# Two graph layers on one core: small products ahead of the first columns, each bucket's norm and tables two groups further up

## The reference, cut to what matters

```python
edge_index = jnp.stack([src, dst])
# first layer: sums over the edges, then a residual norm
w0_features = x @ w0
w1_features = x @ w1
dst, src = (edge_index[0], edge_index[1])
messages = w1_features[src]
neighbours = jax.ops.segment_sum(messages, dst, num_segments=N)
x = _layernorm(x + jax.nn.relu(w0_features + neighbours))
# second layer: attention over the edges, a softmax per destination
h_all = jnp.einsum('nf,rof->rno', x, W).reshape(r, n, h, d)
h_src = h_all[edge_type, src]
h_dst = h_all[edge_type, dst]
scores = jnp.einsum('ehd,hd->eh', h_src, attn_src) + jnp.einsum('ehd,hd->eh', h_dst, attn_dst)
...
x = _layernorm(x + out.reshape(n, h * d))
```

## Time and profile before

| what | value |
|---|---|
| median of 3 runs | 2725.85 us (2725.09 to 2735.58) |
| profiled execution | 2729.65 us, span 2727.8 us |
| mean granted TensorE clock | 0.89 of full speed |
| busy share: TensorE, GpSimd, VectorE, ScalarE | 84%, 68%, 70%, 61% |
| chain that ended last: TensorE, VectorE, GpSimd, issue, DMA | 47%, 16%, 15%, 11%, 7% |

### The profile page before, as it was taken

One profiled execution on the slowest core, in us unless ns is written; L12 is line 12 of the kernel. 1 busy time (PEld: TensorE's weight loads), 2 busy tenths in 40 slices (PEclk: granted clock), 3 DMA queues, 4 the chain that ended last, 5 costly groups with the idle time before them and its releaser, 6 DMA issues.

```text
span 2727.8 us, 38107 instructions
## 1 busy us (share of the span) xinstructions
PE 2283.6 (84%) x9936; PEld 1648.0 (60%) x9936; DVE 1923.1 (70%) x4221; ACT 1656.4 (61%) x3517; POOL 1844.3 (68%) x1875
## 2 busy tenths in 40 slices
PE   8886798999999999999986677777777777777765
PEld 3465576677777777767764455555555555555541
DVE  9993765555555555555552788888888888888887
ACT  4594465566666666666645566666666666666643
POOL 1004777777777777777754777777777777777735
PEclk9996898999999999999997788888787788877888
DMA  5203455854444444444454445444554454444535
GB/s 159 80 5 112 115 158 135 251 175 153 162 154 162 154 152 147 159 155 154 162 122 162 130 140 148 139 139 140 145 142 139 137 148 141 137 139 138 142 91 160
DMA packets 177777, 387.53 MB, mean 142 GB/s; under 512 B 42669, under 2 KB 106867, under 8 KB 171042
## 3 DMA queue, kind: packets, MB, share of 16 engines
q0 software_dynamic: 83888, 233.09, 30.1%
q1 hardware_dynamic: 86626, 99.05, 12.3%
q10 hardware_dynamic: 7056, 52.99, 5.1%
HBM read 302.96 MB, written 82.03 MB: 141 GB/s over the span
## 4 chain that ended last, share of the span: by engine, by line
PE 47%; DVE 16%; POOL 15%; issue 11%; DMA 7%; DVEq 2%; ACT 1%; SPq 0%; POOLq 0%; ACTq 0%; PEldq 0%
PE ps L1689 21%; PE ps L1806 11%; PE ps L1741 10%; POOL region L1337 8%; POOL region L1292 5%; DMA region<-ha_d,idx_t 4%; DVE nodes L884 4%; DMA region<-y_d,edge_z 2%; PE ps L1789 2%; DVE region L873 2%; DVE nodes L766 1%; PE ps L1823 1%; DVE region L612 1%; DMA ha_d<-region 1%; POOL region L1354 1%
## 5 line engine op out<-in xcount | busy, mean ns | idle before, releaser
L1292 POOL DMA_INDIRECT region<-y_d,edge_z x856 | 876.4, 1024 | 448.7 <-issue 239.0
L1337 POOL DMA_INDIRECT region<-ha_d,idx_t x880 | 893.6, 1015 | 306.9 <-issue 246.0
L766 DVE TENSOR_TENSOR nodes<-ps,nodes 128x512 f32 x856 | 591.4, 691 | 512.8 <-PE ps L1689 394.8
L1689 PE MATMUL ps<-region 128*128 128x256 f32 x3424 | 803.0, 388 | 67.6 <-DMA region<-y_d,edge_z 40.1
L1689 PEld LDWEIGHTS ps<-region 128*128 128x128 f32 x3424 | 656.8, 194 | 232.8 <-issue 110.2
L1806 PE MATMUL ps<-region 128*128 128x264 f32 x1760 | 614.9, 480 | 124.3 <-DVE nodes L884 119.3
L1806 PEld LDWEIGHTS ps<-region 128*128 128x128 f32 x1760 | 356.0, 228 | 300.5 <-DVE nodes L884 220.3
L884 DVE TENSOR_TENSOR nodes<-ps,nodes 128x264 f32 x880 | 372.5, 423 | 98.4 <-DVE nodes L884 48.3
L1461 ACT ACTIVATE region<-iota_n,edge_z 128x256 f32<-128x256 f32 x856 | 364.8, 499 | 62.6 <-PE ps L1689 56.4
L1741 PE MATMUL ps<-region,edge_z 128*128 128x512 f32 x784 | 360.4, 593 | 5.7 <-ACT region L1503 4.5
L1556 ACT ACTIVATE region<-region,ones 128x512 f32<-128x512 f32 x220 | 158.8, 722 | 275.4 <-PE ps L1806 270.1
(11 more groups left out here) (264 smaller groups left out, 1848.1 us busy)
## 6 DMA issues: line engine op xcount, KB each, us to landing
ha_d<-region ACTq DMA_DIRECT2D x49, 1056.0 KB
region<-near_d SPq DMA_DIRECT2D x55, 512.0 KB, 5.3
region<-ha_d,idx_t POOLq DMA_INDIRECT x880, 4.2
region<-y_d,edge_z POOLq DMA_INDIRECT x856
edge_z<-level_d SPq DMA_DIRECT2D x55, 136.0 KB, 4.0
kl_d<-region SPq DMA_DIRECT2D x8, 903.0 KB, 9.8
edge_z<-kl_d SPq DMA_DIRECT2D x55, 129.0 KB
y_d<-edge_z SPq DMA_DIRECT2D x25, 256.0 KB, 3.2
```

What stands on the lines that cost most here:

```text
L766: v.tensor_tensor(into, ps[:, u, :], into, ALU.add).then_inc(added0, 1)
L1292: g.indirect_dma_start(rows0[c % RING][:, u, :], None, y_d, bass.IndirectOffsetOnAxis(ap=y_idx[:, k:k + 1], axis=0), bounds_check=node_bou ...
L1337: g.indirect_dma_start(rows[s][:, k, :], None, ha_rows, bass.IndirectOffsetOnAxis(ap=idx_t[:, B * b + k:B * b + k + 1], axis=0), bounds_ch ...
L1689: mm = t.matmul(ps[:, u, h * D:(h + 1) * D], lhsT=sel0[c % SEL][:, u, h * P:(h + 1) * P], rhs=rows0[c % RING][:, u, :], start=True, stop=True)
```

## The change

On TensorE, `small_weights` goes from behind the columns of group 1 to ahead of those of group 0. VectorE's norm of a bucket goes from group done+6 to done+4; `turn_at` and `unit_at` give two groups less for every bucket, on TensorE and, one group behind, on ScalarE. The power on GpSimd, the loads and stores in SP's list and all one-time work keep their groups.

```diff
         def turn_at(t):
 
-            return done_at(t) + (7 if t < BK - 1 else 9)
+            return done_at(t) + (5 if t < BK - 1 else 7)
...
         def unit_at(t, k):
 
-            return done_at(t) + (8 if t < BK - 1 else 16) + 8 * k // 10
+            return done_at(t) + (6 if t < BK - 1 else 14) + 8 * k // 10
...
                     if g == done_at(t) + 1:
                         node_sums(t, jobs[t])
-                    if g == done_at(t) + 6:
+                    if g == done_at(t) + 4:
                         normalise(t)
...
             for c in range(NG + LATE):
+                if c == 0:
+                    small_weights()
                 if c < NG:
                     sum_columns(c)
-                if c == AT["wab"]:
-                    small_weights()
                 if c == AT["firsts"]:
                     first_edges()
```

## The result

The changed kernel takes 2709.64 us (median of 6 runs, 2705.24 to 2712.30), the one before 2725.47 in the same comparison: a ratio of 0.9937, 95% interval 0.9924 to 0.9949, or 17 us less (14 to 21; the two medians lie 15.8 us apart). The forecast was 2697 us, with 2690 to 2713 as its range: faster, as forecast, by 0.6% instead of 1.05%.

What follows compares the result with a forecast made beforehand. The prediction took GpSimd's gathers to bound the first layer, leaving only its standing still and the tail to win. Start 15.0, stores 6.0 and tail 7.6 sum to 28.6 us: 2697 us from the 2725.85 median, range 2690 to 2713.

Steps and rivals of the forecast that it cites:

- the tail: After the first layer's last gathers: fewer table products behind the last columns and an earlier wait win 7.6 us (3.4 to 9.3).
- the stall near 497: GpSimd's 5.3 us wait at 497.64, from a delayed table store; with smaller waits, 6.0 us won (0 to 8.1).
- The new collision: Bucket 1's first table store goes out beside 4-byte stores at 405.68; uncovered, the sum would be lower by 5.3 us.
- The other collision that was named: Bucket 2's other table tile: its store, moved up, now meets SP's large edge stores; no separate size given.
- Slower: Rival: VectorE waits for GpSimd's power in every bucket, delaying the sums; 2740 us, chance 0.05.
- Beyond the cover each us costs 24, once per bucket: VectorE's moved norm waiting for the power: free within a 2 us cover, each us beyond it costs 24 us.
- VectorE waits less than 2 us: Sign that the forecast is right: VectorE's wait for GpSimd's power stays under 2 us per bucket.
- the start: GpSimd's waits at groups 7 and 10 go once the small weights move: 15.0 us won, lower end 9.8.
- from the median it is 2697 us: Last step: the 28.6 us sum, read from one profiled execution, taken off the 2725.85 us median, a gain of 1.05%.
- Start and tail only: Rival: the stall at 497.64 comes back, leaving 15.0 us and 3.4 to 7.6 us; 2703 to 2707 us, chance 0.25.
- The start is eaten later: Rival: GpSimd stands still again between 343 and 500 us; 2713 to 2717 us, chance 0.14 shared with no effect.
- no effect: Rival: a bound other than GpSimd or TensorE hides the gain; chance 0.14 shared with the start being eaten later.

Runs made afterwards that it cites:

- power on VectorE: The changed kernel with the inverse deviation made on VectorE in eleven small operations and no power on GpSimd: 2687.12 us, ratio 0.9862 to the kernel before.
- weights alone: The kernel before with only the small weights moved ahead of the first columns on TensorE: 2714.39 us, ratio 0.9959 to the kernel before.
- after again: The changed kernel measured and profiled once more, unchanged: 2707.41 us, ratio 0.9932 to the kernel before.
- shift alone: The changed kernel with the small weights left behind group 1, so only norm, turn and tables move up: 2712.77 us, ratio 0.9956 to the kernel before.
- The run that moves the last four buckets: The kernel before with norm, turn and tables two groups further up for buckets 21 to 24 only: 2719.82 us, ratio 0.9984 to the kernel before.

## Why the prediction was right, and by how much it was off

**Right: what is the bound.** The pass ends when GpSimd's gathers are through; only its standing still and the tail were to be won. The power on VectorE moves the last gather by 19.7 us, of which 16.0 are the time taken out of GpSimd's queue.

**Right: where the small weights go.** Their products stand in TensorE's wait for the first gather, the waits at groups 7 and 10 are gone. *They fit there with 1.6 us to spare* failed: 13.0 us at the lower clock, not 10.81, and 0.5 us over. The 10.81 of before held both levels already: 24 of the records took 2.75 us there and the same 24 later 5.28. The clause behind it, that group 0 has time until group 1's gather, held (0.42 us).

**Right: the stall near 497.** The term was 6.0 us of 8.1; all 8.1 went. The meeting of the two stores is shown from both sides: it comes back when the table store stays where it was (12.27 us), and goes when the table store or the 4-byte stores move. The new collision that the Trainium skill's rule ("DMA: Bandwidth & Descriptors", section "Issuing engines are not separate DMA queues") threatened did not come here: bucket 1's store went out at 389.19, 3.4 us ahead of the 4-byte stores at 392.57, and landed after 4.2 us. The trace agrees with that rule of the Trainium skill elsewhere: a GpSimd gather issued at 447.17, 0.2 us ahead of SP's 4-byte stores, took 12.54 us, where one in the steady part of before took 5.42.

```profile
447.17 12.54 DMA region<-y_d,edge_z
```

With the weights alone, bucket 1's first store did go out behind the 4-byte stores (396.63 and 389.38) and took 10.79 us, and GpSimd did not stand still for it: that it would be covered was right. The other collision that was named, with SP's large edge stores, came after the change: the store at 464.55 took 9.9 us and the one at 491.68 took 7.8, and GpSimd's ring covered both.

**Mis-sized: the tail**, 7.6 us forecast, 5.6 in the traces, 4.4 (1.6 to 7.4) alone. The 3.4 us of two table products held: from the end of group 213 to the second layer's first gather are 41.5 us after, 45.0 before. The other part, 4.2 us, was 2.2: the forecast set group 210's start some 5 us behind the issue of its last gather, and the gather took 7.2. In after again the last gather held group 213 instead, and the tail is 57.0 us against 60.4 before: the forecast's lower end of 3.4.

**Wrong: the price of the rival "Slower".** *Beyond the cover each us costs 24, once per bucket*: with 3.8 us of wait in 21 buckets that would have been some 40 us. It cost nothing measurable. I had queued VectorE's and TensorE's work behind the wait rightly, but had not asked whether GpSimd is reached: it has five groups of room. The same slip makes the sign *VectorE waits less than 2 us* harmless either way.

**Wrong: from one execution to the median, above all at the start.** Standing still and tail were forecast at 21.0 and 7.6, and the traces show 22.9 and 5.6: the sum of 28.6 us is right for the profiled execution of before, in which 28.5 us were there to win. The mean of three profiled executions of before (2733.8 us) less that of two of after (2707.6) is 26.3 us. The step that failed is *from the median it is 2697 us*: the profiled execution lay 3.8 us above its median, and I carried its whole standing still over. The gain that was timed is 17 us, 9 to 11 less. The term that was too large is the start: 15.0 us were forecast, 11.2 (7.4 to 14.7) were timed with the weights alone, and in the three executions with a fast gather of group 1 the two waits that it counted are only 5.9 to 8.3 us. The shift alone gave 12.0 us (8.2 to 15.8) where 13.6 were forecast. The run that moves the last four buckets has the pass of before up to there, its profiled execution lies at its median (2719.71 and 2719.82), and GpSimd stands still for 15.7 us in it, 7.2 less than in the execution that the prediction read: with a tail of 5 us that leaves some 21 to win. The two parts alone add up to 23 us, together they gave 17 and, in after again, 18.5; with intervals of 3 to 4 us either way this is no clear difference. Where the last 2 to 4 us lie stays open. Chance can explain that all three profiled executions of before lay above their medians while the two of after lie 1 us below theirs, but that is not shown.

**The rivals.** "Start and tail only" gave 2703 to 2707 and comes nearest in time, but for a wrong reason, as the stall did go: the place of 2709.64 inside the range says little for the terms. "The start is eaten later" and "no effect" have no wait in the trace to stand on.

## What to carry to other kernels

A wait priced from a single profiled execution is one draw: profile the same kernel two or three times before its stalls are added up, above all those that hang on one transfer's landing (the two waits at the start were 15 us in two executions and 5.9 to 8.3 in three). Before a wait is priced once per iteration, follow it to the engine that sets the pace; a ring with room turns it into a one-time lag. And when one engine's queue is the bound, take work out of that queue (here a power that adds 0.63 us per bucket) rather than polish what others wait for.

## What the hardware did that was not expected

- A store of table rows (1056 KB) took 10.79 to 13.17 us in four places of before and weights alone where it went out 2.0 to 7.3 us behind SP's stores of single 4-byte elements (10.97 and 12.27 at 5.0 us), and 4.2 to 4.6 us in three places of after where it went out 3.4 to 7.7 us ahead of them. Beside SP's large stores (903 KB) it took 7.8 and 9.9 us in after.
- Between executions of one program, the columns of group 1 on TensorE took 3.73 us at a granted clock of 1.00 or 6.7 at 0.53; ahead of them TensorE had been idle 0.86 us in the one case and 2.74 in the other, both after 12.3 to 12.4 us of idleness and one group.
- The second layer's gathers took 1.012 us (median) in one execution of before and 1.015 in two, the first layer's 1.014, 1.017 and 1.018; 0.003 us is 2.6 us over the 856 gathers of a pass.
- A power of some 0.73 us among GpSimd's gathers delayed the next gather by 0.63 us, with 0.03 us of idle time ahead of it and 0.18 behind it, where 0.30 stands between two gathers; the gather behind it took 1.08 us where others take 1.01.
